# Batch 0 of a DLRM tower: its ninth one-hot field by products, last-batch layers earlier, pairs picked by two engines

## The reference, cut to what matters

```python
e = jnp.stack([tbl_f[ids[:, f]] for f in range(26)], axis=1)       # 2048 x 26 x 128 rows out of 26 tables
combined = jnp.concatenate([e, r_dense_x[:, None, :]], axis=1)     # 27 fields
interact = jnp.einsum('bfd,bgd->bfg', combined, combined)          # 27 x 27 per sample
z = interact[:, TRIU_I, TRIU_J]                                    # the 351 pairs
h = jnp.concatenate([z, r_dense_x], axis=1)
h = jnp.maximum(h @ W_top1 + b_top1, 0.0)                          # 479 -> 512
h = jnp.maximum(h @ W_top2 + b_top2, 0.0)                          # 512 -> 256
y = h @ W_top3                                                     # 256 -> 1
```

## Time and profile before

| | |
|---|---|
| Three timed runs | 384.46, 381.9, 381.5 us; median 381.9 |
| The profiled execution's own time | 383.58 us |
| Its span, first to last instruction | 381.8 us (1.8 us lie around it) |
| Mean granted TensorE clock | 0.955 of full speed |
| Busy share of the span: PE, POOL, DVE, ACT | 89%, 70%, 62%, 49% |
| Indirect DMAs on POOL | 272 of L383 and 4 of L388 |

### The profile page before, as it was taken

One profiled execution on the slowest core, in us unless ns is written; L12 is line 12 of the kernel. 1 busy time (PEld: TensorE's weight loads), 2 busy tenths in 40 slices (PEclk: granted clock), 3 DMA queues, 4 the chain that ended last, 5 costly groups with the idle time before them and its releaser, 6 DMA issues.

```text
span 381.8 us, 12053 instructions
## 1 busy us (share of the span) xinstructions
PE 340.4 (89%) x5340; PEld 245.6 (64%) x5340; DVE 235.5 (62%) x397; ACT 188.6 (49%) x283; POOL 269.0 (70%) x284
## 2 busy tenths in 40 slices
PE   4999898888996999599999999899996999799767
PEld 2677676666774655467677566667665455478666
DVE  6989999796998085369798567468963030303030
ACT  6678554555444353254445363554528246545413
POOL 7877777777777777777777777777777777777000
PEclk9999999999998999699999999999997899979879
DMA  7997233433343324324334323433221222222000
GB/s 188 260 263 218 70 86 93 100 82 86 90 102 80 80 57 97 92 59 101 71 102 95 96 58 76 114 84 80 55 56 52 56 54 54 57 53 55 16 4 0
DMA packets 24067, 33.34 MB, mean 87 GB/s; under 512 B 6463, under 2 KB 17473, under 8 KB 24016
## 3 DMA queue, kind: packets, MB, share of 16 engines
q0 software_dynamic: 8832, 18.11, 18.2%
q1 hardware_dynamic: 15184, 14.47, 16.2%
HBM read 32.55 MB, written 0.01 MB: 85 GB/s over the span
## 4 chain that ended last, share of the span: by engine, by line
PE 42%; POOL 38%; issue 15%; ACT 2%; DMA 1%; POOLq 0%; ACTq 0%
POOL gat L383 37%; PE prod L441 8%; PE prod L443 8%; PE gram L470 7%; PE back L512 6%; PE back L516 4%; PE front L415 4%; PE back L502 2%; DMA gat<-in_tbl,idx 1%; POOL oh_last L388 1%; ACT ct L626 1%; ACT h L651 1%; PE back L497 1%; PE gram L573 0%; PE prod L512 0%
## 5 line engine op out<-in xcount | busy, mean ns | idle before, releaser
L383 POOL DMA_INDIRECT gat<-in_tbl,idx x272 | 263.1, 967 | 83.1 <-issue 81.6
L739 DVE TENSOR_SCALAR ring<-idb,rowid 125x516 fp32r<-125x516 int32 x216 | 145.1, 742 | 9.8 <-PE prod L443 9.4
L441 PE MATMUL prod<-ring,tab_hi 125*128 125x512 f32 x272 | 112.0, 412 | 4.9 <-DVE ring L733 2.2
L443 PE MATMUL prod<-ring,tab_lo 125*128 125x512 f32 x272 | 108.3, 398 | 0.0
L746 DVE COPY z<-gram 128x216 f32<-128x216 f32 x32 | 12.2, 381 | 118.2 <-PE gram L470 118.2
L626 ACT COPY ct<-front 128x512 f32<-128x512 f32 (+2 forms) x80 | 72.0, 959 | 19.3 <-PE front L415 15.7
L470 PE MATMUL gram<-ct 128*32 128x27 f32 x4096 | 57.1, 196 | 12.2 <-issue 9.5
L470 PEld LDWEIGHTS gram<-ct 128*32 128x32 f32 x4096 | 47.3, 109 | 30.3 <-issue 26.4
L441 PEld LDWEIGHTS prod<-ring,tab_hi 125*128 125x128 f32 x272 | 51.8, 191 | 20.7 <-issue 5.3
L443 PEld LDWEIGHTS prod<-ring,tab_lo 125*128 125x128 f32 x272 | 52.0, 191 | 10.3
L415 PE MATMUL front<-ident,gat 128*128 128x128 f32 x272 | 43.6, 286 | 10.9 <-DMA gat<-in_tbl,idx 5.6
(11 more groups left out here) (73 smaller groups left out, 227.3 us busy)
## 6 DMA issues: line engine op xcount, KB each, us to landing
idb<-in_ids_t SPq DMA_DIRECT2D x27, 258.0 KB
gat<-in_tbl,idx POOLq DMA_INDIRECT x272
oh<-in_tbl SPq DMA_DIRECT2D x3, 448.0 KB
...
```

Of the source, the lines that this page charges most:

```text
L383: nc.gpsimd.indirect_dma_start(out=gat[:, t % GS, i, :], out_offset=None, in_=tables[GATHERED[i]][:, :], in_offset=bass.IndirectOffsetOnAx ...
L441: nc.tensor.matmul(prod[:, :], tab_hi[0:OH_P, m, k, :], ring[0:OH_P, k, 0:SB], start=(k == 0), stop=False)
L443: nc.tensor.matmul(prod[:, :], tab_lo[0:OH_P, m, k, :], ring[0:OH_P, k, 0:SB], start=False, stop=(k == OH_K - 1)).then_inc(used, 1)
L739: nc.vector.tensor_scalar(ring[0:OH_P, k, :], idb[0:OH_P, n % IDB, :, 0:IW], rowid[0:OH_P, k:k + 1], None, ALU.is_equal).then_inc(built, 1)
```

## The change

- NX = 0: the ninth field of batch 0 goes by one-hot products like the other eight (one more id spreading, eight more chunks on DVE, 16 more products on PE, one more copy on ACT). POOL issues 17 gathers in every tile, none of L388. In tile 0 the new steps stand behind the last transpose fill, the spreading ahead of the third.
- The steps of the last batch stand elsewhere: blocks of the job before go into gaps behind G or between fills, and of tile 14's job (E) six of seven blocks stand ahead of the last two fills of tile 15, so that only fills, G and the tail are left. The seventh (layer 3) stands in the tail. In tile 4 and tile 8 the second one-hot field stands ahead of the first layer block.
- Fewer waits on PE: no `front_free` for the first two fills of a tile, no `placed` after tile 0, no wait for the Gram banks, no `hi_ready`, one or two waits instead of one per block ahead of layers 2 and 3, and no `bank_clear` where a wait ahead of it covers it.
- The last tile's pairs: DVE turns fields 14 to 26 first, ACT wraps and picks these while DVE turns and picks the rest; PE turns the three thirds into three banks, ACT copies the first and third, DVE the second, and layer 1's first block waits for each third apart.
- SP waits for `gram_done` of two more tiles before it loads the dense rows of batches 2 and 3.

The diff, cut (semaphore names, the call of `pick_last_pairs` and most rows of the order table are left out):

```diff
@@ -34,7 +34,7 @@
 NS = 4
-NX = 1
+NX = 0
 NA = NO - NX
@@ -102,19 +102,21 @@
...
-        return T[0:1] + N[4:5] + T[1:2] + N[5:6] + T[2:3] + Z + T[3:4] + N[6:7] + E[0:3] + T[4:5] + E[3:4] + G + E[4:5]
+        return T[0:2] + Z + E[0:2] + T[2:3] + E[2:6] + T[3:5] + G
...
-        return T[0:2] + O[0:1] + T[2:3] + Z + T[3:4] + J[0:1] + T[4:5] + O[1:2] + G[0:1] + PL + G[1:2] + J[1:2] + G[2:4]
+        return T[0:2] + O[0:1] + T[2:3] + Z + T[3:5] + O[1:2] + J[0:1] + G[0:1] + PL + G[1:2] + J[1:2] + G[2:4]
@@ -137,7 +139,7 @@
-END = [("Z", TILES - 1), ("L", NB, 2, 1), ("L", NB, 3, 0)]
+END = [("L", NB, 3, 0)]
 TAIL = [("L", 1, m) for m in range(M1)] + [("L", 2, m) for m in range(M2)] + [("L", 3, 0)]
@@ -196,6 +198,8 @@
+        zc_last = gat[:, (TILES - 2) % GS, 0:TCH, :].rearrange("p i d -> p (i d)")[:, 0:NPAIR]
         z2 = sb("z2", [P, NF, PITCH])
@@ -286,7 +296,8 @@
         id_rows_f = tab_lo[0:NA, NO - 1, 0:BT, :].rearrange("p k s -> p (k s)")
-        pick_row = tab_hi[0:NA, NO - 1, 0:NA, :]
+        pick_row = tab_hi[0:NA, NO - 2:NO, :, :].rearrange("p m k d -> p (m k) d")[:, 2 * OH_K - NA:2 * OH_K, :]
         ids_homes = [h2[:, 0, :], h2[:, 1, :], zt[:, 2, :]]
@@ -306,6 +317,14 @@
+        def third(k):
+            return (back, prod, gram[:, 2, :])[k][0:ZP, 0:P]
+        def wrap(copy):
+            return copy(z2[:, TOP:NF, NF:PITCH], z2[:, TOP:NF, 0:HALF])
@@ -356,7 +375,9 @@
                         sp.wait_ge(back_done, BACK_INDEX[("L", b - 1, 1, M1 - 1)] + 1)
+                        sp.wait_ge(gram_done, GC * (BT * b + 2))
                         sp.wait_ge(placed, BT * b)
@@ -409,7 +430,8 @@
                 pe.wait_ge(gathered[t % GS][c], 16 * gathers_landed(t, c))
-                if TF * t + c >= 2:
+                if c >= 2:
@@ -432,7 +454,7 @@
                 if b == 0 or (b == 1 and m >= NA):
-                    pe.wait_ge(hi_ready, m + 1)
@@ -457,13 +479,12 @@
                     pe.wait_ge(front_free, TF * (t + 1))
-                    pe.wait_ge(placed, t + 1)
                     if t == 0:
+                        pe.wait_ge(placed, 1)
                         pe.wait_ge(pads_ready, 1)
-                if n >= 4:
-                    pe.wait_ge(gram_dve if c % 2 else gram_act, GC // 2 * (t - 1) + c // 2 + 1)
@@ -477,18 +498,19 @@
+            def last_back(job, n):
+                return max(BACK_INDEX.get(("L", job, n, m), 0) for m in range((M1, M2)[n - 1]))
...
                     return
-                for m in range((M1, M2)[n - 2]):
-                    step = ("L", job, n - 1, m)
-                    if step in PROD_INDEX:
-                        pe.wait_ge(prod_free, NP + PROD_INDEX[step] + 1)
-                    else:
-                        pe.wait_ge(back_free, BACK_INDEX[step] + 1)
+                pe.wait_ge(back_free, last_back(job, n - 1) + 1)
+                last = ("L", job, n - 1, (M1, M2)[n - 2] - 1)
+                if last in PROD_INDEX:
+                    pe.wait_ge(prod_free, NP + PROD_INDEX[last] + 1)
@@ -500,6 +522,14 @@
+            def turn_last_pairs():
+                pe.wait_ge(pairs_ready, TILES)
+                pe.wait_ge(low_picked, 1)
+                pe.wait_ge(back_free, BACK_INDEX[END[0]])
+                pe.wait_ge(prod_free, NP + len(PROD_INDEX))
+                for k in range(ZK):
+                    nc.tensor.transpose(third(k), zc_last[:, k * ZP:(k + 1) * ZP], ident[:, :]).then_inc(last_turned, 1)
@@ -509,6 +539,9 @@
                     for k in range(ZK):
+                        if columns == TAIL_JOB and m == 0:
+                            pe.wait_ge((last_zt_act, last_zt_dve, last_zt_act)[k], (1, 1, 2)[k])
                         ins = nc.tensor.matmul(dst, w1z[0:ZP, k, units], zt[0:ZP, k, lo:hi],
@@ -526,9 +559,11 @@
                     pe.wait_ge(weights_in, 16 * 6)
-                bank_clear(("L", job, n, m))
                 if m == 0:
...
+                if m > 0 or n == 1 or BACK_INDEX[("L", job, n, m)] > last_back(job, n - 1) + 1:
+                    bank_clear(("L", job, n, m))
                 if beside(("L", job, n, m)):
@@ -559,12 +594,9 @@
                 dense_part(tail_banks[m], TAIL_JOB, m)
-            turn_pairs(TILES - 1)
-            layer_step(*END[1][1:])
-            pe.wait_ge(back_free, BACK_INDEX[("Z", TILES - 1)] + 1)
+            turn_last_pairs()
             for m in range(M1):
                 layer_block(tail_banks[m], TAIL_JOB, 1, m).then_inc(tail_done, 1)
-            layer_step(*END[2][1:])
             _, lo, hi = TAIL_JOB
@@ -574,6 +606,8 @@
+            layer_step(*END[0][1:])
             for k in range(M2):
@@ -685,7 +719,8 @@
                         if q[0] == 0:
-                            copy_halves(q[1] + 1)
+                            if q[1] + 1 < NO:
+                                copy_halves(q[1] + 1)
                             if q[1] + 2 < NO:
@@ -704,11 +739,18 @@
                         finish_step(*q)
-            copy_pairs(TILES - 1)
-            finish_step(*END[1][1:])
+            act.wait_ge(low_turned, 1)
+            wrap(nc.scalar.copy).then_inc(low_wrapped, 1)
+            act.wait_ge(low_wrapped, 1)
+            nc.scalar.copy(zc_last[:, TOP * HALF:NPAIR].rearrange("p (g k) -> p g k", k=HALF), windows(z2, TOP, HALF)
+                           ).then_inc(low_picked, 1)
+            for k in (0, 2):
+                act.wait_ge(last_turned, k + 1)
+                nc.scalar.copy(zt[0:ZP, k, SB - P:SB], third(k)).then_inc(last_zt_act, 1)
             for i, (_, n, m) in enumerate(TAIL):
-                if i == M1:
-                    finish_step(*END[2][1:])
+                if i == M1 + M2:
+                    finish_step(*END[0][1:])
                 act.wait_ge(tail_done, i + 1)
@@ -752,13 +794,26 @@
                 dve.wait_ge(z1_turned, t + 1)
-                nc.vector.tensor_copy(z2[:, TOP:NF, NF:PITCH], z2[:, TOP:NF, 0:HALF]).then_inc(z2_wrapped, 1)
+                wrap(nc.vector.tensor_copy).then_inc(z2_wrapped, 1)
                 if t > 0:
...
+            def pick_last_pairs():
+                dve.wait_ge(gram_act, GC // 2 * TILES)
+                dve.wait_ge(gram_dve, GC // 2 * TILES)
+                dve.wait_ge(pairs_ready, TILES - 1)
+                nc.vector.transpose(z2[:, TOP:NF, 0:QUAD], z1[:, :, TOP:NF].rearrange("p g f -> p f g")).then_inc(low_turned, 1)
+                nc.vector.transpose(z2[:, 0:TOP, 0:QUAD], z1[:, :, 0:TOP].rearrange("p g f -> p f g")).then_inc(z1_turned, 1)
+                dve.wait_ge(z1_turned, TILES)
+                nc.vector.tensor_copy(zc_last[:, 0:TOP * HALF].rearrange("p (g k) -> p g k", k=HALF), windows(z2, 0, TOP)
+                                      ).then_inc(pairs_ready, 1)
+                dve.wait_ge(last_turned, 2)
+                nc.vector.tensor_copy(zt[0:ZP, 1, SB - P:SB], third(1)).then_inc(last_zt_dve, 1)
```

17 lines of the change are left out of this document (12 added, 5 removed).

## The result

| | before | after |
|---|---|---|
| Median of 11 executions on the same chip | 383.09 us | 379.07 us |
| Ratio after to before, 95% interval | | 0.9879 [0.985, 0.9909] |
| Lowest and highest | 381.5, 384.46 | 375.29, 384.36 |
| The profiled execution's own time, its span | 383.58, 381.8 us | 384.36, 382.5 us |
| Mean granted TensorE clock of that execution | 0.955 | 0.960 |

The ratio leaves out the three executions of after that lie over 1.5% above its fastest (382.17, 382.6 and 384.36 us, slow ones by that rule); over all eleven the medians give a gain of 4.0 us. The ratio on the 381.9 of the table ahead of the prediction is 377.3, a gain of 4.6 us (3.5 to 5.7), where 8.4 was forecast. The profiled execution of after is the slowest of its eleven, so from tile 12 on a second profile is set beside it: `a0_second`, the changed kernel once more, with an execution of 377.46 us.

What follows compares the result with a forecast made beforehand. Gathers on POOL were taken to bound the kernel, PE after the change: from 383.58 us, G of tile 15 earlier (-6.2) and the tail (-2.2) gave 375.2, less 1.7 for the median 373.5; range 368.5 to 380.5.

Steps and rivals of the forecast that it cites:

- What bounds before: POOL issues gathers without waiting for PE and sets the fourth fill of tile 15, at 354.44; PE's work follows.
- POOL, -5.0: Four gathers fewer at 1.25 us each, so tile 15's fourth fill could be at 349.4.
- Batch 0 on PE, +0.5: Ninth field's products, less idle and half clock at 121.04 to 124.26, leave PE 0.5 us later at 127 us.
- Fewer waits, -1.0 out of 0 to 4: 67 fewer semaphore instructions on PE save 1.0 us, bounds nothing to 4.0.
- The dead stretch: Batch 1: a 4.1 us stop inside a Gram plus half clock, taken as accident, -6.3; rival that it stays, 0.18.
- Last batch on PE: Tiles 14 and 15: moved blocks +5.9, new waits +5.5, old idle and half clock -4.1 before tile 15's fourth fill.
- the 4.1: Stretch 332 to 339: 1.2 us idle and 2.9 us of half clock, counted as going away.
- +5.9 and +5.5: Ahead of tile 15's fourth fill: 5.9 us of moved blocks, 5.5 us of new waits in tiles 14 and 15.
- -6.8 of other terms: PE terms up to tile 12: batch 0 +0.5, fewer waits -1.0, dead stretch -6.3.
- POOL's floor: Tile 15's fourth fill no earlier than 349.4, set by the gathers; as a rival 369.4 us, chance 0.22.
- The tail, -2.2: From G of tile 15 on: one stall less -1.1, pairs -0.3, layer 1 earlier -0.8.
- Slower by the clock: Rival: dead stretch stays and waits for Z drop PE's clock over the moved blocks; 386.8 us, chance 0.04.

Runs made afterwards that it cites:

- v12_old_tail: Changed kernel with the order of tiles 12 to 15 and the tail of the kernel before; 375.38 us, ratio 0.9802 to before.
- v18_waits_only2: Kernel before with only the fewer PE waits and the one-hot field ahead of the first layer block in tiles 4 and 8; 381.62 us, ratio 0.9931.
- v2_nx1: Changed kernel with NX = 1, so batch 0's ninth field is gathered again (four more gathers), tile 0's order as before; 378.38 us, ratio 0.9875.
- v10_order_only: Kernel before with nothing but the new order of tiles 12 to 15, still 276 gathers; 384.0 us, ratio 1.0053.
- v5_warm2: Changed kernel with two unread 128x512 products on PE in the wait ahead of Z in tiles 14 and 15; 376.26 us, ratio 0.9873.
- v15_warm_all2: Changed kernel with unread products in most PE pauses of tiles 14 and 15 and ahead of the last pairs; 375.04 us, ratio 0.975.
- v1_old_order2: Changed kernel with the order of tiles 12 to 15 as in the kernel before, all else changed; 375.17 us, ratio 0.9827.

## Why the prediction was half right

- **What bounds before: right in the main.** POOL issues without a pause and meets PE at the fourth fill of tile 15. `v12_old_tail` without the gathers has that fill at 349.23 (forecast floor 349.4). But the prediction has PE behind POOL all the way from 121.04 to there, and it is not. In tile 14 it waits for a gather too:

```profile
333.31 1.65 PE L415 MATMUL front<-ident,gat 128*128 128x128 f32 x5 [1.14 <-DMA gat<-in_tbl,idx]
```

That wait is nearly all of the 1.21 idle in 332 to 339, which the prediction took for idle time of PE's order.
- **POOL, -5.0: right.** `v12_old_tail` to `v18_waits_only2`, that is with and without the ninth field in the old order: 0.9802 to 0.9931, 1.3% or 4.9 us (some 2.6 to 7.3 by their intervals). In the new order G is 4.2 later with the gathers (`v2_nx1`). `gather(3)` began at 73.78 (forecast 73.4), tile 1 was turned at 71.3 (forecast 72.1).
- **Batch 0 on PE, +0.5: right.** Tile 4 begins 4.2 later (116.71 to 112.51 before); its wait and the half clock behind it are gone.
- **Fewer waits, -1.0 out of 0 to 4: too small, inside its bounds.** `v18_waits_only2` is 0.69% (0.3 to 1.1) under before, 2.6 us with the moved fields of tiles 4 and 8.
- **The dead stretch, an accident: right as to its length.** A stop of 4.1 is gone in after, and also in `v10_order_only` and `v18_waits_only2`, where the longest such stop is 2.1 and 1.7. The place is not an accident: `v2_nx1` stops there too, 1.48 at 153.87. Its worth depends on the gathers: `v10_order_only` begins tile 12 4.4 earlier than before (283.65), but with 276 gathers it is held at the fourth fill there until 290.73, 1.25 ahead of before's 291.98.
- **Last batch on PE, the step that failed.** It is the half clock that the sum put at nothing: "so I keep the 4.1 as a gain but leave the new waits at their full price". The moved work and the new waits came about as forecast (+5.9 and +5.5; the waits are 1.96, 0.66, 0.55 in tile 15 and 1.87, 0.66 in tile 14). The old half clock at 332 to 339 went, and in the profiled execution its place was taken by one at 328.84 to 335.67 and one at 352.73 to 359.56, each right behind a pause ahead of Z. The prediction had seen that the new idle places spoke for a new half clock, and priced it at 1.6 apiece only in a sentence beside the sum; with 6.17 of PE's work in each, half of it, 3.1, is what one costs. The profiles show how the time goes with it. From the fourth fill of tile 12 to the last fills of tile 15 (forecast 68.3, that is 61.0 before, +5.9, +5.5, -4.1) the new order took, in the six profiles at some 380 us that have it,

| profile | us | of it at half clock |
|---|---|---|
| v5_warm2 | 66.83 | 0 |
| v15_warm_all2 | 68.33 | 3.4 |
| v10_order_only | 69.42 | 6.6 |
| a0_second | 69.93 | 6.8 |
| v2_nx1 | 70.56 | 7.6 |
| after | 77.15 | 22.3 |

  Each us at half clock adds 0.4 to 0.5 us, and little else is left over. The pauses ahead of Z are in all six, filled with unread products or not, so the rival that they were longer than priced falls. In `v15_warm_all2` the last fills are at 354.51 and G at 356.46 (forecast 353.5 and 355.8), and its ratio, 0.975, times 381.9 is 372.4 us, beside 373.5: what is missing in the changed kernel is this term and, behind G, the same one over layer 1.
- A second error stands behind it. The forecast compared the new order with the old one at before's lateness. With -6.8 of other terms the old order is back under POOL's floor: the profile of `v12_old_tail` has half clock at 286.96 to 293.78 and 327.92 to 331.33, and PE still waits 2.86 for the fourth fill of tile 15, so what these stretches cost counted for nothing. The new order gives up this cover: its PE never waits for a gather behind tile 12, so the clock it loses there counts (the table above). That this cover is the whole of the old order's lead is not shown: at one mean clock, 0.982, `v1_old_order2` took 373.44 and 374.74 us and the changed kernel 377.46 to 378.75. By my own numbers the new order was worth 1.2 (G at 355.8 in place of 356.95); it measured +2.0 alone (`v10_order_only`) and, by ratios whose intervals partly overlap, +1.9 to +2.9 in the changed kernel (0.9877 less 0.9827 or 0.9802). In the profiles of `a0_second` and `v12_old_tail` a third of it lies ahead of G (358.12 and 357.42), the rest behind (17.5 and 16.3 to the end).
- **The tail, -2.2: right in its parts for the new order, but for the clock.** One stop in G in place of two. From G's end to layer 1: 5.6 before, 4.69 in `v10_order_only` (366.77 to 371.46), 3.7 with the split pick, so the pick and copies brought 1.0 (forecast 1.1). G's start to the end is 17.4 (forecast 17.6), but with layer 1 at half clock (+1.3), which the range held and the sum did not. In the old order the split pick brings nothing (`v1_old_order2` beside `v12_old_tail`), as PE is busy with tile 14's blocks there. And the 19.8 of before was a draw as well: the old tail took 16.8 in `v18_waits_only2` and 16.3 in `v12_old_tail`.
- **The rivals.** POOL's floor is what the old order gives, not this change. "Slower by the clock" named the mechanism, and the point from which it decides (G later than 364.2) was passed in the profiled execution, 365.09; its other half, the dead stretch, did not come.

The Trainium skill (TensorE: Matmul & The Clock Gate, section A second HAM failure mode: psum-queue depth-cycling) tells, of a bf16 kernel, of short idle times between groups of matmuls that make the gate swing between its levels. The runs here agree: right ahead of the six half-clock stretches between tile 12 and the last layers in after and `a0_second` stand pauses of 1.67 to 2.19 us, and in `v15_warm_all2`, with the pauses of tiles 14 and 15 filled, there is one stretch of 3.4 us (at 287.61) between tile 12's start and the end of the last layer. A pause of this length does not always bring one: behind 1.90 at 285.26 and 1.69 at 325.22 in `a0_second` the clock stayed full.
